# Score maxima in three bf16 terms, and another order on TensorE around their turn

## What is computed

```python
qh, kh, vh = proj(q, Wq, bq), proj(k, Wk, bk), proj(v, Wv, bv)   # q = layernorm(x), k = v = ctx
qh, kh, vh = (interfere(qh), interfere(kh), interfere(vh))        # 16 heads, 4 x 4 mix in each
scores = jnp.einsum('bhqdm,bhkdm->bhqkm', qh, kh) / math.sqrt(dk)
weights = jax.nn.softmax(scores, axis=3)
out = jnp.einsum('bhqkm,bhkdm->bhqdm', weights, vh)               # then out @ Wo.T + bo
x = x + attention(...)
w = sc[g_idx] * (wq - (zq + 1)[g_idx])                            # both FFN weights, GPTQ 4 bit
x = x + (silu(gate) * up) @ w_d                                   # of layernorm(x) @ w_gu
```

## Time and profile before

| | before |
|---|---|
| median of 3 runs | 871.94 us (868.27 to 872.51) |
| profiled execution, its time | 870.51 us |
| its span (first to last instruction) | 868.8 us |
| TensorE busy | 792.7 us, 91% |
| VectorE busy | 488.0 us, 56% |
| ScalarE busy | 427.9 us, 49% |
| GpSimd busy | 297.3 us, 34% |
| mean granted TensorE clock | 0.933 of 2.4 GHz |
| setup, until the first keys | about 88 us |
| a loop chunk | 85.7 us |

### The profile page before, as it was taken

One profiled execution on the slowest core, in us unless ns is written; L12 is line 12 of the kernel. 1 busy time (PEld: TensorE's weight loads), 2 busy tenths in 40 slices (PEclk: granted clock), 3 DMA queues, 4 the chain that ended last, 5 costly groups with the idle time before them and its releaser, 6 DMA issues.

```text
span 868.8 us, 24146 instructions
## 1 busy us (share of the span) xinstructions
PE 792.7 (91%) x10116; PEld 565.1 (65%) x10119; DVE 488.0 (56%) x1000; ACT 427.9 (49%) x817; POOL 297.3 (34%) x297
## 2 busy tenths in 40 slices
PE   5455778899999999999999999999999999999898
PEld 5411324465788578857885787578767876786484
DVE  9978663543656465746564656466646654554321
ACT  1656665452655265526652665266526662565120
POOL 2155455232145214521453144304430543054020
PEclk9655665999999999999999999999999999999899
DMA  8943223000010101011001100120011000100000
GB/s 276 264 119 88 59 73 85 26 3 2 26 29 3 50 27 29 3 51 35 21 3 49 46 9 3 51 53 2 3 49 53 2 3 25 29 3 14 13 2 24
DMA packets 21512, 37.04 MB, mean 43 GB/s; under 512 B 4158, under 2 KB 8414, under 8 KB 21404
## 3 DMA queue, kind: packets, MB, share of 16 engines
q1 hardware_dynamic: 21404, 35.48, 14.1%
HBM read 26.47 MB, written 4.19 MB: 35 GB/s over the span
## 4 chain that ended last, share of the span: by engine, by line
PE 70%; DVE 14%; issue 7%; ACT 7%; POOL 1%; DVEq 0%; ACTq 0%; POOLq 0%
PE bank L556 17%; PE bank L571 13%; PE bank L527 10%; PE bank L537 9%; PE bank L697 4%; PE bank L714 3%; DVE nmf L1275 3%; PE bank L583 3%; PE bank L690 3%; ACT arena L918 3%; PE bank L504 2%; PE bank L671 2%; DVE stats L1212 1%; DVE arena L1207 1%; DVE small L1060 1%
## 5 line engine op out<-in xcount | busy, mean ns | idle before, releaser
L556 PE MATMUL bank<-arena,WGU 128*128 128x256 f16 (+1 forms) x2112 | 248.4, 275 | 1.4 <-DVE arena L762 1.4
L556 PEld LDWEIGHTS bank<-arena,WGU 128*128 128x128 f16 (+1 forms) x2112 | 206.9, 101 | 28.1 <-DVE arena L762 1.7
L1463 POOL TENSOR_TENSOR arena<-arena 128x512 f16<-128x512 f32 x128 | 147.0, 1177 | 207.2 <-ACT arena L925 207.2
L571 PE MATMUL bank<-WD,arena 128*128 128x512 f16 (+1 forms) x528 | 121.0, 379 | 0.0
L918 ACT ACTIVATE arena<-bank,small 128x512 f32<-128x512 f32 x128 | 89.2, 776 | 54.9 <-PE bank L697 54.9
L1453 POOL TENSOR_TENSOR arena<-arena 128x512 f16<-128x512 f32 (+1 forms) x48 | 51.8, 1078 | 172.2 <-ACT arena L901 172.2
L527 PE MATMUL bank<-arena,WT 128*128 128x256 f16 x768 | 90.9, 281 | 2.9 <-DVE arena L762 2.5
L527 PEld LDWEIGHTS bank<-arena,WT 128*128 128x128 f16 x768 | 77.1, 101 | 16.3 <-issue 4.2
L537 PE MATMUL bank<-WT,arena 128*128 128x512 f16 x384 | 86.8, 383 | 0.0
L571 PEld LDWEIGHTS bank<-WD,arena 128*128 128x128 f16 (+1 forms) x528 | 49.3, 97 | 53.3
L1275 DVE TENSOR_REDUCE nmf<-bank 128x8 f32<-128x512 f32 x128 | 79.3, 681 | 5.6 <-PE bank L671 5.4
(11 more groups left out here) (172 smaller groups left out, 1002.2 us busy)
## 6 DMA issues: line engine op xcount, KB each, us to landing
arena<-in_L_ffn_qweight_gu SPq DMA_DIRECT2D x8, 688.0 KB, 5.5
arena<-arena SPq DMA_DIRECT2D x32, 144.0 KB, 2.7
WT<-in_ctx SPq DMA_DIRECT2D x8, 512.0 KB, 9.7
arena<-in_ctx SPq DMA_DIRECT2D x8, 512.0 KB, 3.7
arena<-in_x SPq DMA_DIRECT2D x8, 512.0 KB, 3.9
out_y<-arena SPq DMA_DIRECT2D x16, 256.0 KB, 2.0
arena<-in_L_ffn_qweight_down SPq DMA_DIRECT2D x10, 256.0 KB, 3.5
arena<-in_L_xattn_Wk SPq DMA_DIRECT2D x1, 1024.0 KB, 5.8
```

The source lines that it names most:

```text
L556: mm = e.matmul(pb[0:m, i * TOK:(i + 1) * TOK], WGU[:, sp, kb, half * INTER + fb * P:half * INTER + fb * P + m], x2T[:, mp, kb, :], start= ...
L571: mm = e.matmul(pb[:, :], hT[0:m, sp, fb, t * P:(t + 1) * P], WD[0:m, mp, fb, :], start=(n == 0), stop=(n == 3 * FB - 1))
L1463: e.tensor_tensor(phl[:, a, 1, :], pring[:, a, :], phl[:, a, 0, :], ALU.subtract).then_inc(S["p_lo"], 1)
```

## The change

1. The maxima are cut into three bf16 terms on VectorE (`dve_split_max`, four dependent operations after each batch's maxima). `nm16` holds three terms and zeros, so that the turned tile has term and group on its partitions; `nmT` and `sel` are bf16, and a selector column picks all three terms of its group. The turn is a bf16 matmul with `ident16`, into JB[1] instead of AB[0].
2. On TensorE, the turned scores are issued as soon as the maxima are done, ahead of the turn. The turn waits for the split. FFN slice 1 follows, then the first tile's transposes (they now come after `nm_ready`, since they use the same bank), then the selector matmuls, in a function of their own (`pe_add_max`).
3. The maximum over the partitions in setup is a transpose of `MX`, a VectorE maximum of 11 rows, a diagonal 11 x 11 matrix and a matmul with ones, issued on TensorE ahead of the transposes of Wo. ScalarE's first weight waits for `wscale_ready`, ahead of the other factors.
4. The statistics of the first chunk, and their reciprocal square roots on GpSimd, come after the stretch w0. The load of x comes after the first two pieces of 4-bit weights.

```diff
+LAST_EXTRA = ("", "cT1", "cT1", "xT1")
-        nmf = sb("nmf", [P, 4, 32], F32)
-        nmT = sb("nmT", [P, P], F32)
-        sel = sb("sel", [P, KB, P], F32)
+        nmf = sb("nmf", [P, 4, 8], F32)
+        nrest = sb("nrest", [P, 4, 8], F32)
+        nm16 = sb("nm16", [P, 4, 4, 8], BF16)
+        nmT = sb("nmT", [P, P], BF16)
+        sel = sb("sel", [P, KB, P], BF16)
...
-            e.dma_start(xin, x_d[0]).then_inc(S["x_loaded"], 16)
             load_piece(e, 0)
             load_piece(e, 1)
+            e.dma_start(xin, x_d[0]).then_inc(S["x_loaded"], 16)
...
                 if w == 3:
+                    pe_all_max(e)
                     e.wait_ge(S["wo_permuted"], 1)
...
+        def pe_all_max(e):
+
+            e.wait_ge(S["fold_evicted"], 3)
+            e.wait_ge(S["max_ready"], 1)
+            e.transpose(AB[0][0:11, 0:P], MX, ident[:, :]).then_inc(S["max_turned"], 1)
+            e.wait_ge(S["max_diag"], 1)
+            e.matmul(AB[1][:, 0:11], ones[:, :], max_diag[:, :], start=True, stop=True).then_inc(S["max_all"], 1)
...
                 e.wait_ge(S["t_lo"], t_at(c, name) - 1)
+                e.wait_ge(S["nm_ready"], NB * c + b + 1)
...
+                pe_scores_turned(e, c, b)
                 pe_turn_max(e, c, b)
-                pe_extras(e, c, EXTRAS[b][0])
                 ffn_slice(slot[1])
-                pe_scores_turned(e, c, b)
+                pe_extras(e, c, b, EXTRAS[b][0])
+                pe_add_max(e, c, b)
                 if b:
                     pe_values(e, c, 2 * b - 1)
...
         def pe_turn_max(e, c, b):
 
+            name = LAST_EXTRA[b]
+            if isinstance(c, int) and c == 0 and b == 0:
+                pass
+            elif b == 0:
+                e.wait_ge(S["t_lo"], t_at(c - 1, "oT1"))
+            elif name in (T_LAST if is_last(c) else T_ORDER):
+                e.wait_ge(S["t_lo"], t_at(c, name))
+            e.wait_ge(S["nm_split"], NB * c + b + 1)
+            e.matmul(JB[1][:, 0:P], nm16[:, :, :, :].rearrange("p a k n -> p (a k n)"), ident16[:, :],
+                     start=True, stop=True).then_inc(S["nm_turned"], 1)
+
+        def pe_scores_turned(e, c, b):
+
             e.wait_ge(S["max_done"], SLOTS * c + 4 * b + 4)
-            e.transpose(AB[0][:, 0:P], nmf[:, :, :].rearrange("p a n -> p (a n)"), ident[:, :]).then_inc(S["nm_turned"], 1)
-
-        def pe_scores_turned(e, c, b):
-
-            e.wait_ge(S["nm_ready"], NB * c + b + 1)
...
+        def pe_add_max(e, c, b):
+
+            e.wait_ge(S["nm_ready"], NB * c + b + 1)
...
+            e.wait_ge(S["wscale_ready"], 1)
+            act_whi(e, 0)
             e.wait_ge(S["scale_ready"], 1)
-            act_whi(e, 0)
...
-            e.activation(nmT[:, :], AB[0][:, 0:P], ACT.Copy).then_inc(S["nm_ready"], 1)
+            e.activation(nmT[:, :], JB[1][:, 0:P], ACT.Copy).then_inc(S["nm_ready"], 1)
...
-            e.wait_ge(S["x_loaded"], 16)
-            for t in range(TILES):
-                ln_stats(e, "x", 0, t, xin[:, t, :])
+            e.wait_ge(S["max_turned"], 1)
+            link(e, e.tensor_reduce(max_col[:, :], AB[0][0:11, 0:P], AX_X, ALU.max))
+            e.tensor_scalar(max_diag[:, :], ident[0:11, 0:11], max_col[:, 0:1], None, ALU.mult).then_inc(S["max_diag"], 1)
             e.wait_ge(S["max_all"], 1)
+            link(e, e.tensor_copy(MR, AB[1][:, 0:11]))
...
             dve_ticks(e, "w0")
+            e.wait_ge(S["x_loaded"], 16)
+            for t in range(TILES):
+                ln_stats(e, "x", 0, t, xin[:, t, :])
             dve_hot_d(e)
...
+        def dve_split_max(e, c, b):
+
+            step = 3 * (NB * c + b)
+            e.wait_ge(S["max_done"], SLOTS * c + 4 * b + 4)
+            reached(e, S["nm_turned"], NB * c + b)
+            e.tensor_copy(nm16[:, :, 0, :], nmf[:, :, :]).then_inc(S["nm_step"], 1)
+            e.wait_ge(S["nm_step"], step + 1)
+            e.tensor_tensor(nrest[:, :, :], nmf[:, :, :], nm16[:, :, 0, :], ALU.subtract).then_inc(S["nm_step"], 1)
+            e.wait_ge(S["nm_step"], step + 2)
+            e.tensor_copy(nm16[:, :, 1, :], nrest[:, :, :]).then_inc(S["nm_step"], 1)
+            e.wait_ge(S["nm_step"], step + 3)
+            e.tensor_tensor(nm16[:, :, 2, :], nrest[:, :, :], nm16[:, :, 1, :], ALU.subtract).then_inc(S["nm_split"], 1)
...
                     dve_max(e, c, 4 * b + a)
+                dve_split_max(e, c, b)
                 dve_slot(e, c, slot[0], first)
...
-            e.wait_ge(S["max_ready"], 1)
-            e.partition_all_reduce(MR, MX, P, ABSMAX).then_inc(S["max_all"], 1)
-            pool_ln(e, "x", 0)
             pool_ticks(e, "scales")
             e.wait_ge(S["fold_done"], 4)
             e.memset(vv_words, 0.0).then_inc(S["vv_zeroed"], 1)
             pool_ticks(e, "w0")
+            pool_ln(e, "x", 0)
             pool_ticks(e, "w1")
```

More of the change, by code:

```diff
@@ L244, in build @@
         MX = maxima[:, 0, 0:11]
+        max_col, max_diag, ones = sb("max_col", [11, 1], F32), sb("max_diag", [11, 11], F32), sb("ones", [11, P], F32)
         MR = maxima[:, 1, 0:11]
@@ L270, in build @@
             "t_ready", "wmax_done", "wo_permuted", "fold_done", "fold_evicted", "bias_done", "bias_evicted",
-            "max_ready", "max_all", "scale_ready", "whi_done", "wlo_done",
+            "max_ready", "max_turned", "max_diag", "max_all", "wscale_ready", "scale_ready", "whi_done", "wlo_done",
             "scw_loaded", "zw_loaded", "wide_ready", "zwide_ready", "sc_table", "z_table", "maxq_ready", "maxq_all", "scq_ready",
@@ L281, in build @@
             "t_hi", "t_lo", "qk_evicted", "qm_ready", "v_evicted", "v_hi", "v_lo",
-            "jrow_ready", "sel_ready", "max_done", "nm_turned", "nm_ready",
+            "jrow_ready", "sel_ready", "max_done", "nm_step", "nm_split", "nm_turned", "nm_ready",
             "st_done", "exp_done", "p_hi", "p_lo", "o_step", "o_ready",
@@ L505, in pe_transpose_tile, with pe_extras @@
             mm.then_inc(S["tr_done"], 1)
-        def pe_extras(e, c, names):
+        def pe_extras(e, c, b, names):
             for name in names:
@@ L645, in pe_chunk @@
                 ffn_slice(slot[2])
-                pe_extras(e, c, EXTRAS[b][1])
+                pe_extras(e, c, b, EXTRAS[b][1])
                 ffn_slice(slot[3])
@@ L999, in dve_setup @@
             e.memset(MXQ, 0.0)
+            e.memset(ones[:, :], 1.0)
             link(e, e.memset(NHALF, -0.5))
@@ L1011, in dve_setup @@
             e.wait_ge(S["gm_ready"], 1)
-            link(e, e.tensor_scalar(LIFT, GM, 8.0, 100.0, ALU.is_ge, ALU.mult))
+            link(e, e.tensor_scalar(LIFT, GM, 24.0, 100.0, ALU.is_ge, ALU.mult))
             link(e, e.tensor_tensor(KEY, smalli[:, 7:8], LIFT, ALU.add))
@@ L1016, in dve_setup @@
                             ALU.is_equal).then_inc(S["sel_ready"], 1)
-            e.memset(nmf[:, :, :], 0.0)
+            e.memset(nm16[:, :, :, :], 0.0)
             for k in range(2):
@@ L1082, in dve_setup @@
             link(e, e.tensor_scalar(PW.bitcast(I32), BD.bitcast(I32), 0x7F800000, None, ALU.bitwise_and))
-            link(e, e.tensor_scalar(SC.bitcast(I32), PW.bitcast(I32), -1.0, float((254 + TOP) << 23), ALU.mult, ALU.add))
+            e.tensor_scalar(SC.bitcast(I32), PW.bitcast(I32), -1.0, float((254 + TOP) << 23), ALU.mult, ALU.add).then_inc(S["wscale_ready"], 1)
+            e.wait_ge(S["wscale_ready"], 1)
             link(e, e.tensor_scalar(IV.bitcast(I32), PW.bitcast(I32), float(-(TOP << 23)), None, ALU.add))
@@ L1274, in dve_max @@
             e.wait_ge(S["s_done"], SLOTS * c + s + 1)
-            e.tensor_reduce(nmf[:, a, 0:8], AB[a][:, :].rearrange("p (n k) -> p n k", n=8), AX_X, ALU.max,
+            e.tensor_reduce(nmf[:, a, :], AB[a][:, :].rearrange("p (n k) -> p n k", n=8), AX_X, ALU.max,
                             negate=True).then_inc(S["max_done"], 1)
+        def dve_split_max(e, c, b):
[9 more added lines that the diff above has]
+            e.tensor_tensor(nm16[:, :, 2, :], nrest[:, :, :], nm16[:, :, 1, :], ALU.subtract).then_inc(S["nm_split"], 1)
         def dve_stats_next(e, c):
```

## The result

| | before | changed |
|---|---|---|
| median | 870.11 us (868.22 to 872.51, 4 runs) | 857.37 us (857.23 to 858.77, 4 runs) |
| ratio | | 0.9859, interval 0.9834 to 0.9883 |
| span of the profiled execution | 868.8 us | 857.0 us |

A forecast was written before the change was run, and what follows sets the result against it. TensorE's own work plus its waits was taken to bound loop chunks. Savings of 13.3 (loop), 2.5 (chunk 0) and 2.8 (chunk 7) less 0.1 (setup) made 18.5 us, giving 853 us; range 844 to 863, the forecast's own 849 to 858.

The forecast's parts named there:

- TensorE's sum: TensorE's work in a batch where nobody waits: 3.04 to 2.24 us, 0.80 saved, of which 0.73 from the selectors.
- The waits: TensorE's waits in loop chunks: batch 1 from 1.09 to about 1.6, a new 0.4 for outputs, batch 2 stays 0.44.
- Loop: Loop chunks 1 to 6: 2.22 us saved in each, 13.3 us in all.
- chunk 0: First chunk, with stand-in FFN work and a 2.25 us wait for batch 1's maxima: 2.5 us saved.
- chunk 7: Last chunk, no tiles before the selectors in batches 0 to 2: 0.9, 0.3, 0.8 and 0.8, 2.8 us saved.
- The tail: End of a loop chunk: slack before values of slots 12 and 13 need GpSimd's residues shrinks from 0.7 to 0.25, holds.
- Setup: Work before the chunks: 0.1 us later in sum, bounds 2 earlier and 2 later.
- two terms: In setup: dequantisation starts 2.0 us early; statistics ahead of the one-hot table add 2.1 in full to TensorE's 7.07 wait.
- (1): Rival: TensorE's waits in loop chunks do not grow, 3.2 us and more saved per chunk, 845 us; chance 0.15.
- (2): Rival: the clock falls inside the loop after the new waits, 1.6 us in each of six chunks, 863 us; chance 0.15.
- (3): Rival: bf16 brings nothing, selectors keep the fp32 ones' 0.99 us per batch, 871 us; chance 0.05.
- (4): Rival: VectorE becomes the bound, the split's 0.84 us lying open in all 32 batches, 899 us; chance 0.04.

The follow-up runs named there:

- The order alone: Kernel before with only TensorE's new step order and the turn in JB[1]; maxima, turn and selectors stay fp32, no split: 877.35 us, ratio 1.0073.
- the setup alone: Kernel before with only the changed setup, its batches left as they were: 870.03 us, ratio 1.0000.
- one term: Changed kernel with only the first bf16 term of the maxima, so the split is one cast, in the new order: 852.11 us, ratio 0.9778.
- the outputs first: Changed kernel with VectorE's normalised outputs put ahead of the FFN eviction behind the split: 860.78 us, ratio 0.9877.
- the terms alone: Kernel before with only the three bf16 terms, bf16 turn and bf16 selectors, in the old order, the turn waiting for the split: 882.48 us, ratio 1.0139.
- one term in the old order: Kernel before with bf16 turn and selectors in the old order, the maximum cut to its first term (one cast): 855.54 us, ratio 0.9835.
- three kernels: Changed kernel with both statistics moves (848.94 us), the same with the tile behind the selectors (847.62), and the loop's statistics move with that tile order (849.43).
- a fourth: Changed kernel with the next chunk's statistics moved from batch 0 to the end of batch 1: 849.63 us, ratio 0.9748.
- the first experiments: Early follow-up runs, timed on the same chip as the kernel before; the text does not list which.

## Why the prediction was right, and where not

**TensorE's sum was the term that was mis-sized.** The prediction had 0.80 saved per batch, 3.2 per chunk; busy time fell by 2.26. The type brought what it should: selectors of 0.33 against 0.95 to 0.99, and 0.22 directly behind the turned scores. But I priced each step by its row in the old order. Three prices came out dearer at their new places: the turn 0.16 to 0.18 (taken: 0.10, between nothing and the old 0.17; the fp32 turn takes 0.26 at this place, so the type brought 0.1 and the place took it back), the selectors 0.33 behind the tile (0.26), and the ctx and x tiles ahead of the selectors 0.55 to 0.57 (0.44). For the selectors the neighbour in front shows as the reason: the same matmuls take 0.22 directly behind the turned scores. For the tiles it does not: the second tile of the same batches takes 0.44 behind the same kind of FFN matmuls, and what made the first one dearer stays open. And the saving in batch 3 starts from 2.97, not batch 0's 3.04. Per chunk that is about 0.28, 0.28, 0.25 and 0.1, together the 0.9 that is missing. The order alone shows such costs by themselves: 0.87 of work more with nothing taken away. In six chunks it makes 5.6 us, of which smaller waits gave some back: the loop as a whole fell short by 5.0 of the 6.7 us that the sum missed. The forecast had allowed some 2 us for the selectors and nothing for the turn and the tiles. That the time still lies within 849 to 858 it owes to the width taken for the split, setup and the spread of runs, not to this term.

**The waits went as said, a little smaller.** Exponentials of batch 0: 0.24 earlier in the chunk (33.65 us after its start before, 33.41 now), forecast 0.3. Wait in batch 1: 1.34, forecast 1.6, since TensorE came less early. Split 0.88, forecast 0.84; turn 0.93 after the last maximum, forecast 0.9. New wait for the outputs: 0.28, and 0.61 to 0.65 in odd chunks, forecast 0.4. Together the waits grew by 0.72 in chunk 2 and by 1.05 in chunk 1 (2.58 against 1.53), forecast 0.98.

**Chunk by chunk.** Loop 8.3 instead of 13.3; chunk 0 1.75 instead of 2.5, with the wait of 2.25 grown to 2.51 and the low clock behind it as before; chunk 7 1.4 instead of 2.8, for the same prices, with waits of 0.23 and 0.17 for outputs and, which the forecast had at nothing, of 0.22 and 0.20 for the split. The tail held: in chunk 2 no values of slots 12 and 13 wait for GpSimd.

**Setup: right in sum, with two terms too large by about the same amount.** Timelines of the changed kernel around the reduction, against the earlier trace rows:

```profile
36.76 0.37 PE L470 MATMUL bank<-ident,maxima 128*11 128x128 f32 x1 [9.92 <-DVE maxima L1092]
...
38.29 0.48 PE L457 MATMUL bank<-ident,arena 128*128 128x128 f32 x1
38.40 0.17 DVE L1098 COPY maxima<-bank 128x11 f32<-128x11 f32 x1 [0.69 <-PE bank L472]
...
44.45 1.99 ACT L854 ACTIVATE WT<-arena,small 128x2048 f16<-128x2048 f32 x1
...
76.13 0.48 PE L501 MATMUL bank<-WD,arena 68*128 68x352 bf16 x1 [8.55 <-DVE arena L1241]
```

VectorE goes on at 38.40 (forecast 38.5), Wk is scaled at 44.45 (44.0), 1.56 earlier and not 2.0; the wait under the one-hot table grew by 1.48 and not 2.1. They cancel, and the setup alone measured 1.0000. By the rule of the Trainium skill ("GPSIMD Engine Reference", section 4.1 Engine selection), which gives a reduction over partitions to GpSimd, I had reckoned 2 us worse: the trace does not agree. Two matmuls and two small VectorE operations took 1.79 from the last maximum to its use (36.61 to 38.40), the reduction there 3.52; and the interval of the setup alone, 0.9984 to 1.0015, leaves no room for 2 us more (1.0023).

**The rivals.** (1) fell: both waits are there. (2) did not happen in the changed kernel, whose loop keeps 1.00 behind 1.34; but it was a near thing. With one term the clock fell once behind 1.70, with the outputs first once behind 1.51, and with the terms alone three times in six behind 1.97. The Trainium skill's pattern ("TensorE: Matmul & The Clock Gate", section A second HAM failure mode: psum-queue depth-cycling) of short idles that bring the clock down thus shows here in other orders of the same work; it cost 1.2 to 1.5 us each time. The rival's ladder, by which a longer wait brings the lower clock, does not hold: in chunk 0 the clock fell behind 2.25 and 2.51, but with one term in the old order a wait of 2.56 left it at 1.00, and with the terms alone one of 3.23 did. TensorE's timeline there, and the table of stretches right behind it:

```profile
174.71 0.22 PE L684 MATMUL bank<-ident,nm 128*128 128x128 bf16 x1 [3.23 <-DVE nm L1293]
...
174.70:178.00 3.30, 3.29 (x97) 2.18 (x98) 1.24 (x6) 1.67 (x4) 0.00 (x0) 1.00 0.02 5
```

(3) fell, by the 0.33 and 0.22. (4) is real as a mechanism: the terms alone are it, with 0.70 to 0.99 more on the path in each batch and 1.4% lost, the lower clock included. What kept it away is the piece that I credited in the sum, the turned scores over the split.

## What to carry to other kernels

When an engine's steps are reordered, price each by a row in which the same kind of work stands directly around it, or keep a bound for every new place; here that was 0.9 us per chunk. Two halves of a change can each lose and still win together, when one makes a delay and the other covers it, so test both alone and ask of each new dependent operation what runs over it. Where the bounding engine's longest wait ends with another engine, look in that engine's queue for work that nobody needs yet: moving 1.95 us of statistics by one batch brought about 1%, more than half of what the change itself did.

## What the hardware showed that I had not expected

- The price of short matmuls depends on their place. Sixteen bf16 selectors took 0.22 directly behind other 32-row matmuls and 0.33 behind 128-row ones; the fp32 ones 0.95 and 1.10. Four fp32 transposes took 0.44 behind 512-column matmuls, 0.44 to 0.50 behind an fp32 turn, 0.51 to 0.65 behind a bf16 turn, and behind 256-column fp16 matmuls 0.44 as a second tile but 0.55 to 0.57 as a first one, so that the shape in front does not set it alone.
- The length of a wait did not decide the clock. With the terms alone, a wait of 1.97 in each of six alike chunks was followed by a fall in three. Waits of 1.03 and 0.67 in chunk 0 (1.04 and 0.68) were followed by a fall in three kernels and not in a fourth, from which one of the three differs only in the tile's place. In chunk 0 the clock fell after 2.25 and 2.51 and stayed after 2.56 and 3.23; after 1.34 it never fell in the changed kernel's loop. Executions of one kernel differ in the same way: of the kernel before, those timed beside the first experiments at a mean clock of 0.937 to 0.939 took 867.4 to 869.4 us, those at 0.933 took 870.4 to 872.5.
- Setup moved by 1.8 us between profiled executions of kernels with the same setup (first Q projection at 142.64 to 144.47), and chunk 0 took 63.0 or 65.0 as the clock went. A forecast of a setup term below 2 us can't be judged from a pair of profiles; the timed 1.0000 judged it.
